# One pair of VectorE scale instructions merged, three engines' steps reordered, and one matrix's set-up moved behind the first two tiles

## The reference

```python
xn = _layernorm(x)
# attention
q, k, v = split(xn @ W_qkv.T)            # 16 heads of 16
q = softmax(q, axis=-1) * HEAD_DIM ** -0.5
k = exp(k)
context = exclusive_cumsum_over_buckets(einsum('bhnsd,bhnse->bhnde', k, v))
den = einsum('bhnsd,bhnd->bhns', q, exclusive_cumsum_over_buckets(sum(k)))
attn = einsum('bhnsd,bhnde,bhns->bhnse', q, context, 1 / maximum(den, 1e-6))
# feed-forward, fq: blocks of 16, scale = max(max|block| / 6, 1e-12), values rounded to the FP4 grid
h = silu(fq(xn) @ fq(w_gate).T) * (fq(xn) @ fq(w_up).T)      # 704 wide
out = x + attn @ W_out.T + fq(h) @ fq(w_down).T
```

## Time and profile before

| | before |
|---|---|
| median of 3 runs | 1360.32 us (1359.64 to 1360.74) |
| profiled execution, its own time | 1361.72 us |
| its span, first to last instruction | 1360.0 us |
| PE busy | 1271.1 us, 93% |
| DVE busy | 1309.7 us, 96% |
| ACT busy | 969.4 us, 71% |
| POOL busy | 355.0 us, 26% |
| mean granted TensorE clock | 0.989 of full speed |

### The profile page before, as it was taken

One profiled execution on the slowest core, in us unless ns is written; L12 is line 12 of the kernel. 1 busy time (PEld: TensorE's weight loads), 2 busy tenths in 40 slices (PEclk: granted clock), 3 DMA queues, 4 the chain that ended last, 5 costly groups with the idle time before them and its releaser, 6 DMA issues.

```text
span 1360.0 us, 41012 instructions
## 1 busy us (share of the span) xinstructions
PE 1271.1 (93%) x9934; PEld 871.0 (64%) x9934; DVE 1309.7 (96%) x3901; ACT 969.4 (71%) x3221; POOL 355.0 (26%) x791
## 2 busy tenths in 40 slices
PE   0279999999999999999999999999999999999996
PEld 0157666666666666666666666666666666666664
DVE  6869999999999999999999999999999999999996
ACT  1567777777777777777777777777777777777772
POOL 2212223222222323222222222223232222323220
PEclk9889999999999999999999999999999999999998
DMA  4024544444454444444544444545454454445444
GB/s 129 12 40 82 108 98 100 105 100 102 98 114 100 101 105 98 103 100 98 113 101 105 98 102 99 112 98 104 105 109 99 92 115 101 96 105 110 97 83 91
DMA packets 432380, 133.64 MB, mean 98 GB/s; under 512 B 397404, under 2 KB 431836, under 8 KB 432348
## 3 DMA queue, kind: packets, MB, share of 16 engines
q1 hardware_dynamic: 431622, 132.60, 46.8%
q10 hardware_dynamic: 726, 0.72, 0.2%
HBM read 19.99 MB, written 16.78 MB: 27 GB/s over the span
## 4 chain that ended last, share of the span: by engine, by line
DVE 52%; issue 33%; DVEq 7%; PE 5%; ACT 2%; DMA 1%; SPq 0%; ACTq 0%
DVE hx_v L880 7%; DVE ga L810 5%; DVE blk L834 3%; DVE xring L963 3%; DVE hx_v L887 3%; DVE h L820 2%; DVE drec L794 2%; DVE xq_s L935 2%; DVE q_rows L922 2%; DVE att L799 2%; DVE osum L958 2%; DVE blk L843 1%; DVE dz L786 1%; DVE hrow L854 1%; DVE dmx L790 1%
## 5 line engine op out<-in xcount | busy, mean ns | idle before, releaser
L418 POOL TENSOR_TENSOR xn_s<-xn,xn_s 128x256 f16<-128x256 f32 x128 | 108.6, 848 | 820.3 <-ACT xn_s L535 820.3
L1165 PE MATMUL outp<-w_down_cat,q_rows 128*128 128x256 f16 x1408 | 246.1, 274 | 0.0
L617 ACT ACTIVATE snap<-ctxp,mask 64x68 f32<-64x68 f32 x1024 | 236.5, 310 | 3.3
L1165 PEld LDWEIGHTS outp<-w_down_cat,q_rows 128*128 128x128 f16 x1408 | 138.3, 98 | 16.5
L1167 PE MATMUL outp<-w_down_lo,q_rows 128*128 128x256 f16 x640 | 147.6, 274 | 0.0
L580 ACT ACTIVATE th<-unit0a,c_g 128x352 f32<-128x352 f32 x128 | 71.0, 554 | 97.3 <-PE unit0b L1078 95.3
L556 ACT ACTIVATE qexp<-qsh,c_q 128x256 f32<-128x256 f32 x128 | 65.1, 508 | 99.0 <-DVE qsh L773 98.8
L580 ACT ACTIVATE th<-unit1a,c_g 128x352 f32<-128x352 f32 x128 | 71.0, 555 | 87.4 <-PE unit1b L1078 65.0
L827 DVE TENSOR_REDUCE blk<-h 128x44 f32<-128x704 f32 x128 | 123.8, 967 | 0.1
L411 POOL TENSOR_TENSOR att_s<-att,att_s 128x256 f16<-128x256 f32 x128 | 87.9, 687 | 108.1 <-ACT att_s L572 108.1
L880 DVE TENSOR_TENSOR hx_v<-h,blk 128x704 f32<-128x704 f32 x128 | 111.0, 868 | 0.0
(11 more groups left out here) (199 smaller groups left out, 4059.0 us busy)
## 6 DMA issues: line engine op xcount, KB each, us to landing
xring<-x SPq DMA_DIRECT2D x128, 128.0 KB, 2.7
out<-xring SPq DMA_DIRECT2D x128, 128.0 KB, 2.5
xnt<-xn_s SPq DMA_TRANSPOSE x128, 2.5
xqt<-xq_s SPq DMA_TRANSPOSE x128, 2.4
att_t<-att_s SPq DMA_TRANSPOSE x128, 2.5
q_rows<-q_rows SPq DMA_TRANSPOSE x128, 3.6
raw_qkv<-wqkv_t SPq DMA_DIRECT2D x1, 768.0 KB, 4.4
raw_up<-wup ACTq DMA_DIRECT2D x2, 352.0 KB
```

The source lines that it names most:

```text
L418: nc.gpsimd.tensor_tensor(xn_s[:, par, 1, :], xn[:, par, :], xn_s[:, par, 0, :], ALU.subtract).then_inc(xn_lo, 1)
L617: nc.scalar.activation(kept[:, :, cols], sums[:, :, cols], ACT.Copy, scale=mask[rows, f, h:h + 1])\
L1165: nc.tensor.matmul(downp, hqt[:, par, m, :], w_down_cat[:, m, :], start=(m == 0), stop=False)
```

## The change

1. **DVE, fewer instructions.** `block_scales` makes the scales of x and of h in one instruction (`scalar_tensor_tensor` over 60 columns) instead of two `tensor_scalar`. The floor, which was a constant for x and a value per row for h, now comes from a new tile `blk_floor`, filled once in the set-up by one memset and one copy. The new instruction counts a semaphore of its own, `blk_scaled`.
2. **DVE, order.** `max_q` goes ahead of `block_scales`; the first part of `add_up` stands between `block_scales` and `over_one`, the second part behind `over_row`. The two roundings then follow each other directly.
3. **PE, order.** `transpose_q` goes from ahead of `project_att` to the end of the step.
4. **ACT, order.** `snapshot` goes from the end of the step to between the two tanh; `squares_of` goes ahead of `copy_qt`, which is now last.
5. **Set-up.** The down matrix's transpositions and their copies stand behind step(0, 0) and step(0, 1) and go through the bank `outp` alone, so that each of the six groups waits for the copy of the one before it.

```diff
@@ step on ACT @@
                 tanh_gate(k, 0, par)
+                snapshot(k + 1)
                 normalise_waits(k + 3)
                 mean_waits(n, d + 4)
                 tanh_gate(k, 1, par)
                 factor_of_row(k - 1, odd)
                 normalise(n, d + 3)
                 mean_of(n, d + 4)
+                squares_wait(k + 4)
                 high_xn(k + 3, odd)
-                squares_wait(k + 4)
+                squares_of(n, d + 4)
                 copy_qt(k + 1, odd)
-                squares_of(n, d + 4)
-                snapshot(k + 1)
@@ set-up on ACT @@
+            for d in range(2):
+                step(0, d)
             for i, (dst, parts) in enumerate(((w_down_cat[:, 0:4, :], P), (w_down_cat[:, 4:8, :], P),
...
-                src = prep_banks[i % 4][:, :].bitcast(fp16)[0:parts, 0:dst.shape[1] * D]
+                src = outp[:, :].bitcast(fp16)[0:parts, 0:dst.shape[1] * D]
                 nc.scalar.activation(dst, src.rearrange("k (m n) -> k m n", n=D), ACT.Copy).then_inc(prep_ev, 1)
-            for n in range(0, 2):
-                for d in range(2):
-                    step(n, d)
+            for d in range(2):
+                step(1, d)
@@ block_scales on DVE @@
-                if is_tile(u):
-                    dve.wait_ge(xq_step, after(u, 6, 1))
-                    nc.vector.tensor_scalar(xblk[:, 1, :], xblk[:, 0, :], SIX_TIE * 2.0 ** 11, XS * TINY * 2.0 ** 11, ALU.mult, ALU.max)\
-                        .then_inc(xq_step, 1)
-                if is_tile(t):
-                    dve.wait_ge(hq_step, after(t, 9, 1))
-                    nc.vector.tensor_scalar(hblk[:, 1, :], hblk[:, 0, :], SIX_TIE * 2.0 ** 11, h_floor[:, :], ALU.mult, ALU.max)\
-                        .then_inc(hq_step, 1)
+                do_h, do_x = is_tile(t), is_tile(u)
+                if do_h:
+                    dve.wait_ge(hq_step, after(t, 8, 1))
+                if do_x:
+                    dve.wait_ge(xq_step, after(u, 5, 1))
+                if do_h or do_x:
+                    both = slice(0 if do_h else FB, FB + XB if do_x else FB)
+                    nc.vector.scalar_tensor_tensor(blk[:, 1, both], blk[:, 0, both], SIX_TIE * 2.0 ** 11, blk_floor[:, both],
+                                                   ALU.mult, ALU.max).then_inc(blk_scaled, 1)
@@ step on DVE @@
                 block_max_h(k - 1, odd)
+                max_q(k + 1, odd)
                 block_scales(k - 1, k + 2)
-                max_q(k + 1, odd)
+                add_up(n, d - 3, 0)
                 over_one(k - 1, k + 2)
                 row_scale(k - 1)
                 shift_q(k + 1, odd)
                 over_row(k - 1)
+                add_up(n, d - 3, 1)
                 over_scales_h(k - 1, odd)
                 over_scales_x(k + 2, par)
                 round_hx(k - 1, k + 2, 0)
-                add_up(n, d - 3, 0)
                 round_hx(k - 1, k + 2, 1)
-                add_up(n, d - 3, 1)
@@ set-up on DVE @@
+            nc.vector.memset(blk_floor[:, FB:FB + XB], XS * TINY * 2.0 ** 11).then_inc(factors, 1)
+            dve.wait_ge(factors, 12)
+            nc.vector.tensor_copy(blk_floor[:, 0:FB], h_floor[:, :].broadcast_to([P, FB])).then_inc(factors, 1)
@@ step on PE @@
                 gate_up(k, 1, par)
-                transpose_q(k + 1, odd)
                 project_att(k - 2, par)
                 project_h(k - 2, par)
+                transpose_q(k + 1, odd)
@@ set-up on PE @@
+            pe.wait_ge(proj_lo, 2)
+            pe.wait_ge(prep_ev, 8)
+            for d in range(2):
+                step(0, d)
             pe.wait_ge(mat_hi[2], 2)
...
-                pe.wait_ge(prep_ev, 8 + i - 3)
-                bank = prep_banks[i % 4][:, :].bitcast(fp16)
+                pe.wait_ge(prep_ev, 8 + i)
+                bank = outp[:, :].bitcast(fp16)
...
-            for n in range(0, 2):
-                for d in range(2):
-                    step(n, d)
+            for d in range(2):
+                step(1, d)
```

More of the change, by code:

```diff
@@ L295, in turn_xq @@
                     return
-                sp.wait_ge(xq_step, after(t, 6))
+                sp.wait_ge(xq_step, after(t, 5))
                 sp.sem_inc(sp_turn, 1)
@@ L306, in turn_h @@
                     return
-                sp.wait_ge(hq_step, after(t, 9))
+                sp.wait_ge(hq_step, after(t, 8))
                 sp.sem_inc(sp_turn, 1)
@@ L520, in normalise_waits @@
                 if begun(t - 2):
-                    act.wait_ge(xq_step, after(t - 2, 6, 3))
+                    act.wait_ge(xq_step, after(t - 2, 5, 2))
             def normalise(n, d):
@@ L585, in scales_x @@
                     return
-                act.wait_ge(xq_step, after(t, 6, 2))
+                act.wait_ge(blk_scaled, t + 1)
                 nc.scalar.activation(xs_hi[:, :].rearrange("p (b i) -> p b i", i=2), twice(xblk[:, 1, :]), ACT.Copy)\
@@ L592, in factor_of_row @@
                     return
-                act.wait_ge(hq_step, after(t, 9, 4))
+                act.wait_ge(hq_step, after(t, 8, 3))
                 if begun(t - 2):
@@ L600, in scales_h @@
                     return
-                act.wait_ge(hq_step, after(t, 9, 5))
+                act.wait_ge(hq_step, after(t, 8, 4))
                 nc.scalar.activation(hs_hi[:, :].rearrange("p (b i) -> p b i", i=2), twice(hblk[:, 1, :]), ACT.Copy,
@@ L818, in times_up @@
                 if begun(t - 2):
-                    dve.wait_ge(hq_step, after(t - 2, 9, 6))
+                    dve.wait_ge(hq_step, after(t - 2, 8, 5))
                 nc.vector.tensor_tensor(h[:, par, half * FH:(half + 1) * FH], ga[:, half, :],
@@ L852, in over_one @@
                 if do_h:
-                    dve.wait_ge(hq_step, after(t, 9, 2))
+                    dve.wait_ge(blk_scaled, t + 4)
                     nc.vector.tensor_reduce(hrow[:, 0, :], hblk[:, 1, :], AX.X, ALU.max).then_inc(hq_step, 1)
@@ L856, in over_one @@
                     if do_x:
-                        dve.wait_ge(xq_step, after(u, 6, 2))
+                        dve.wait_ge(blk_scaled, u + 1)
                     both = slice(0 if do_h else FB, FB + XB if do_x else FB)
@@ L862, in row_scale @@
                 if is_tile(t):
-                    dve.wait_ge(hq_step, after(t, 9, 3))
+                    dve.wait_ge(hq_step, after(t, 8, 2))
                     if begun(t - 1):
@@ L871, in over_row @@
                     return
-                dve.wait_ge(hq_step, after(t, 9, 4))
+                dve.wait_ge(hq_step, after(t, 8, 3))
                 nc.vector.reciprocal(hrow[:, 2, :], hrow[:, 1, :]).then_inc(hq_step, 1)
@@ L920, in scale_h @@
                 else:
-                    dve.wait_ge(hq_step, after(t, 9, 7))
+                    dve.wait_ge(hq_step, after(t, 8, 6))
                 nc.vector.tensor_tensor(rows(hq_s[:, par, part * F:(part + 1) * F]), rows(hx_q[:, 0:F].bitcast(fp16)),
@@ L929, in scale_x @@
                 dve.wait_ge(hx_step, hx_after(t, 3))
-                dve.wait_ge(xq_step, after(t, 6, 4))
+                dve.wait_ge(xq_step, after(t, 5, 3))
                 if begun(t - 2):
```

13 lines of the change are left out of this document (7 added, 6 removed).

## The result

The changed kernel takes **1378.6 us** (median of 4 runs, 1377.9 to 1379.4); the kernel before took 1360.5 on the same chip (1359.6 to 1360.9). The ratio is 1.0134, with an interval of 1.0117 to 1.0152: **slower by 18 us**, where 17 us less were forecast. The time lies outside the forecast's range.

What follows compares the result with a forecast made beforehand. DVE was taken as the bound by 2% (9.90 us a step), PE right behind (9.67). Steps of 9.73 put the last max_q at 1310.7 (-15.7), with the end -17.4: 1344.3 profiled, 1343 us median; range 1335 to 1358.

Steps and rivals of the forecast that it cites:

- the two neighbouring roundings: In DVE's step, the second rounding waits for the first's end: 0.12 us a step added, the roundings 0.70 us apart.
- The merged instruction: In DVE's step, one instruction for both block scales adds 0.13 us a step, between 0.10 and 0.22.
- The term of 0.50: In DVE's step, the old pair of block scales costs 0.50 us a step, which the merging takes away.
- DVE's step: DVE's time per loop step falls from 9.90 to 9.65 us, or 9.86 if the whole contention comes back.
- rival A: In the loop, POOL holds the new block-scale instruction: 9.83 us a step, 1355 us; chance 0.20.
- `add_up` earlier, `transpose_q` last: In the loop, PE's 0.55 us wait for the output bank goes; both moves themselves cost nothing.
- `snapshot` between the tanh: In ACT's step, tanh, normalisation and POOL's low_xn come some 0.8 us later; costs nothing in the loop.
- The start: With the down matrix behind the first pair, max_q of step(1, 0) starts near 104.2, not 98.85: 5.3 us lost.
- The end: PE's last but one use of the output bank and the chain behind it come earlier: 1.7 us won.
- C: In the loop, POOL's L418 falls on DVE's first scaling of x every step: 9.95 us, 1370 us; chance 0.10.
- B: The loop is held elsewhere, at 9.86 us a step and over, so nothing is won: 1358 to 1363 us; chance 0.08.
- DVE's share below 99%: Sign that the forecast is right: in the loop DVE has small waits for PE at max_q, busy below 99%.

Runs made afterwards that it cites:

- e2: The changed kernel with the second rounding's wait for the first rounding moved behind its two other waits; 1356.3 us.
- e6: The changed kernel with the two block scales as two instructions again, in the changed order; 11 us faster than the changed kernel.
- e1: The changed kernel with the second part of add_up put back between the two roundings as a filler; 1346.4 us.
- e10: e8 with transpose_q ahead of project_att again, as before the change; 1334.9 us, 0.9815 of the kernel before.
- e4: The kernel before with the new orders of ACT and PE alone, DVE and set-up as before; slower than the kernel before by 8 us.
- e7: The kernel before with DVE's changes alone, ACT, PE and set-up as before; slower than the kernel before by 60 us.
- e3: The changed kernel with the old set-up, the down matrix transposed through four banks ahead of step(0, 0); 8 us faster than the changed kernel.
- e8: The changed kernel with the second part of add_up between the roundings and with the old set-up; 1337.6 us.

## Why the prediction was wrong

**The step that failed** is the price of the two neighbouring roundings: "0.12 us a step is added, since the second rounding waits for the end of the first". Measured: 0.31 us (1.210 - 0.896), 0.19 more than the term, and e2 takes just these 0.19 away. The wait for the end of the first rounding is there and costs its 0.12 (0.695 - 0.576 in e2). The rest is a cost that the prediction put at nothing: the term was read from the earlier trace rows in an unrolled step, with constant counts, while in the loop two waits with counts from registers stand behind the one that ends last. The kernel showed the order of the three waits, and the bounds given (0 and 0.12 for other such pairs) had no room for it. 124 x 0.19 = 23 us.

*The merged instruction* is the second term that was too small: 0.13 us was taken, with 0.10 to 0.22; measured 0.263, above the upper bound. Its duration, 209 ns, was as forecast, but `osum` starts 0.21 and 0.31 us after it in turn, up to 0.10 us behind its end. Why is open: `osum` has two waits ahead of it, but in e6, with the same two waits, it follows the h scale after 0.15 us. 124 x 0.13 = 16 us. The term of 0.50 it took away was 0.476.

*DVE's step* was to be 9.65, and the working took 9.73 for PE. With the two terms as measured it would have been 9.65 + 0.19 + 0.13 = 9.97, against 9.993 measured. So DVE stayed the bound, PE never showed its floor, and the 0.08 between 9.65 and 9.73, which the prediction allowed for PE, did not exist here. 124 x (9.993 - 9.73) = 32.6 us of the 35.6 by which the forecast missed. That e1's step is 9.729, what the prediction took, confirms less than it seems. With the filler back, its terms give DVE 9.90 - 0.50 + 0.13 = 9.53, but in e1 DVE is as full as before (99.48 us of 100): POOL holds the merged instruction there (342 ns on average), as rival A had it. The agreement is in part luck.

*`add_up` earlier, `transpose_q` last:* right in that PE's wait for the bank went. The order has a small price on PE: from q's transpositions to the qkv matmuls it takes 701.78 - 701.50 = 0.28 us, where it takes 0.22 us ahead of `project_att` if nothing is waited for; the forecast had counted the step's time unchanged. Timeline of PE, changed kernel:

```profile
701.50 0.44 PE L1108 MATMUL trp<-ident,qexp 128*128 128x128 f32 x2
701.78 0.38 PE L1081 MATMUL unit1a<-w_qkv,xnt 128*128 128x512 f16 x1
```

Undoing it (e10) shortened the step by 0.004 us, so this price was worth next to nothing there.

*`snapshot` between the tanh* "costs nothing in the loop": as part of ACT's and PE's orders it costs 8 us in e4 and gives 51 between e7 and e3. Both come through POOL's phase (above), which the prediction saw as a rival and not as a term.

*The start:* 5.3 us lost was forecast; 6.2 came, and against the same orders the move costs 9.2. Of its parts, ACT's pair ended at 92.11 (forecast 91.2) and its six copies were over at 100.97, 8.9 us (forecast 9.4). Timeline of ACT, first, second and last copy:

```profile
92.11 1.01 ACT L665 ACTIVATE w_down_cat<-outp 128x1024 f16<-128x1024 f16 x1
...
94.24 1.02 ACT L665 ACTIVATE w_down_cat<-outp 128x1024 f16<-128x1024 f16 x1 [1.13 <-PE outp L1225]
...
100.59 0.38 ACT L665 ACTIVATE w_down_lo<-outp 64x256 f16<-64x256 f16 x1 [0.51 <-PE outp L1225]
```

The second copy waits 1.13 us for eight transpositions into the one bank, work that was hidden before.

*The end:* 1.7 us were forecast, 0.1 came. The mechanism did hold: from h's last block maxima on DVE to PE's use of the bank passed 1346.38 - 1341.81 = 4.57 us before and 2.82 after, 1.75 less. Most of it was given back by TensorE's clock. PE's timeline at its last use of the bank, changed kernel, and windows of the stretches behind, changed kernel and kernel before, with the same matmul before:

```profile
1362.46 0.37 PE L1081 MATMUL outp<-w_out,att_t 128*128 128x256 f16 x1 [3.01 <-DVE xring L967]
...
1368.83 0.37 PE L1081 MATMUL outp<-w_out,att_t 128*128 128x256 f16 x1 [1.19 <-DVE xring L967]
```

```profile
1368.50:1371.50 3.00, 2.67 (x13) 1.96 (x14) 0.18 (x1) 0.00 (x0) 0.00 (x0) 0.50 0.31 74
```

```profile
1352.00:1355.50 3.50, 2.77 (x23) 2.18 (x23) 0.54 (x2) 0.00 (x0) 0.00 (x0) 1.00 0.32 75
```

```profile
1352.60 0.27 PE L1074 MATMUL outp<-w_out,att_t 128*128 128x256 f16 x1 [1.19 <-DVE xring L963]
```

Before, the last group of products ran at the full clock (2.4 GHz, 0.27 us a matmul); after, most of it ran at half (1.2 GHz, 0.42 us), behind the same wait of 1.19 us. From the last but one `osum` on DVE to the last passed 1355.41 - 1351.45 = 3.96 us before and 1373.01 - 1367.68 = 5.33 after: 1.4 us. In the group ahead of it the granted clock was 0.50 in both kernels; why it was back at 1.00 in time in the one and not in the other was not tried.

**The rivals.** A (POOL holds the merged instruction) did not come in the changed kernel. Its group from 300 to 1300 us, and POOL's timeline ahead of the L851 shown above at 705.28:

```profile
L851 DVE SCALAR_TENSOR_TENSOR blk<-blk,blk_floor 128x60 f32<-128x60 f32 x100 | 20.9, 209 | 0.0
```

```profile
704.62 0.67 POOL L413 TENSOR_TENSOR att_s<-att,att_s 128x256 f16<-128x256 f32 x1
```

POOL ends at 705.29, just as the merged instruction starts. The contention came in e1 and e8, at 342 and 341 ns. C (POOL on the first scaling of x in each step) did not come either: that instruction lasts 289 ns. B named the step from 9.86 on, but with PE held, and it was DVE. So the time came out slower for a reason that none of the cases had; what the forecast lacked was a rival in which DVE's own new neighbours cost more than the row said. One sign that it named did show it: the roundings were to be 0.70 us apart and are 0.88. DVE's share below 99%, listed as a sign of success, came too, but DVE's waits were for itself.

## What to carry to other kernels

Price two neighbouring dependent instructions from a row inside the loop, not from an unrolled step, and read the waits ahead of them. Where several stand there, try the one that ends last in the last place: in this loop that was worth 22 us. In the unrolled steps of the same kernel it cost 0.10 us each, so measure it. Before merging two small instructions, ask which of them is the filler of another's latency. And where POOL's instructions stretch those of another engine, the worth of a reordering cannot be summed from its parts: it decides what POOL's instructions fall on, so look for the groups whose mean duration changed without any change of their own.

## What was not expected of the hardware

- Two waits already met, with counts from registers, behind one that ends last, cost 0.19 us in the loop (0.884 against 0.695). In an unrolled step, with constant counts, the same order gives 0.70 us and the other one 0.80.
- A filler of 0.40 us between the roundings makes them dearer by only 0.576 + 0.395 - 0.884 = 0.09 us than none at all with the changed kernel's order of waits; with e2's order it would be 0.28 us.
- POOL's 0.67 us subtraction made a DVE instruction over 704 columns last 1.8 times as long (911 ns on average in e7, 519 undisturbed), and small ones of 16 columns 0.64 instead of 0.17 us. In the timelines looked at, the held instruction ended with POOL's or behind it.
